# Layer 1's combine: the low half of a weight part one group of gathers later in GpSimd's program

## The reference

```
x = x + gnn(layernorm(x), adj)      # Wh = h @ W; masked softmax of (Wh@a1)_i + (Wh@a2)_j; elu(att @ Wh)
x = x + ffn(layernorm(x))           # router, top 2 of 8, out = sum over 2 experts of weight * (act(t@w1+b1)@w2+b2)
```

## Time and profile before

| | us |
|---|---|
| median of 3 runs | 1663.62 (1662.15 to 1683.7) |
| profiled execution, its own time | 1662.98 |
| its span, first to last instruction | 1661.2 |
| graph stage of layer 1 with the combine | about 578 to 930 |
| expert stage of layer 1 | about 1061 to 1580 |

### The profile page before, as it was taken

One profiled execution on the slowest core, in us unless ns is written; L12 is line 12 of the kernel. 1 busy time (PEld: TensorE's weight loads), 2 busy tenths in 40 slices (PEclk: granted clock), 3 DMA queues, 4 the chain that ended last, 5 costly groups with the idle time before them and its releaser, 6 DMA issues.

```text
span 1661.2 us, 31445 instructions
## 1 busy us (share of the span) xinstructions
PE 1157.8 (70%) x9230; PEld 923.0 (56%) x9231; DVE 992.0 (60%) x1742; ACT 554.3 (33%) x1103; POOL 751.4 (45%) x718
## 2 busy tenths in 40 slices
PE   5888481789999824545546563789989888989910
PEld 3666370478888712433435451477767676767710
DVE  3677698657777632555555798444444443434467
ACT  3776476222222213434446652022212221222200
POOL 2322274155555372444441473255656565655510
PEclk9999755589999956777778555589999998999965
DMA  8110141045555631222220341112222122212279
GB/s 246 47 33 14 45 175 53 14 133 158 163 160 164 149 104 45 60 67 64 64 64 14 127 165 38 39 64 71 74 73 80 66 75 69 76 66 73 67 261 364
DMA packets 124186, 161.23 MB, mean 97 GB/s; under 512 B 27352, under 2 KB 103648, under 8 KB 123872
## 3 DMA queue, kind: packets, MB, share of 16 engines
q1 hardware_dynamic: 97248, 87.10, 15.9%
q0 software_dynamic: 26880, 73.44, 14.9%
HBM read 97.57 MB, written 62.91 MB: 97 GB/s over the span
## 4 chain that ended last, share of the span: by engine, by line
PE 45%; issue 24%; DVE 9%; another core or an unknown queue 8%; DMA 4%; ACT 4%; POOL 3%; SPq 2%; DVEq 0%; ACTq 0%; POOLq 0%
PE bank L762 17%; PE bank L748 16%; PE bank L722 4%; PE bank L734 4%; DMA arena<-expert_outputs 2%; PE bank L607 2%; DVE X L1022 2%; PE bank L635 1%; DMA X<-in_x 1%; DVE stats L1012 1%; POOL stage_w L469 1%; ACT b_bc L814 1%; ACT arena L936 1%; POOL no_edge L478 1%
## 5 line engine op out<-in xcount | busy, mean ns | idle before, releaser
L552 POOL DMA_INDIRECT arena<-split_tokens,gather_row x288 | 288.8, 1003 | 234.2 <-DVE gather_row L1292 94.0
L936 ACT ACTIVATE arena<-bank,b1T 128x256 f32<-128x256 f32 x432 | 173.5, 474 | 629.5 <-PE bank L748 288.7
L762 PE MATMUL bank<-WREG,arena 128*128 x2592 | 332.8, 281 | 54.6 <-issue 35.5
L748 PE MATMUL bank<-arena,WREG 128*128 128x256 f16 x2592 | 327.1, 281 | 12.0 <-issue 11.3
L762 PEld LDWEIGHTS bank<-WREG,arena 128*128 128x128 f16 x2592 | 253.7, 100 | 113.7 <-issue 78.7
L748 PEld LDWEIGHTS bank<-arena,WREG 128*128 x2592 | 254.6, 101 | 51.6 <-issue 18.6
L1304 DVE CAST arena<-arena 128x512 f16<-128x512 f32 (+1 forms) x144 | 85.4, 593 | 250.9 <-ACT arena L936 196.7
L561 POOL DMA_INDIRECT expert_outputs<-arena,scatter_row x144 | 155.5, 1080 | 175.8 <-DVE arena L1317 145.7
L607 PE MATMUL bank<-wg_sb,arena 128*128 128x258 f32 x512 | 160.2, 459 | 93.1 <-issue 40.7
L607 PEld LDWEIGHTS bank<-wg_sb,arena 128*128 128x128 f32 x512 | 111.4, 229 | 125.7 <-issue 53.0
L494 POOL DMA_INDIRECT WREG<-expert_outputs,pos_i x128 | 124.3, 971 | 59.1 <-issue 36.9
(11 more groups left out here) (163 smaller groups left out, 1361.5 us busy)
## 6 DMA issues: line engine op xcount, KB each, us to landing
expert_outputs<-arena SPq DMA_DIRECT2D x72, 256.0 KB
split_tokens<-arena SPq DMA_DIRECT2D x32, 512.0 KB, 2.8
arena<-expert_outputs SPq DMA_DIRECT2D x32, 512.0 KB, 7.5
X<-in_x SPq DMA_DIRECT2D x16, 512.0 KB, 6.0
stage_w<-in_L_ffn_W SPq DMA_DIRECT2D x16, 512.0 KB
out<-X SPq DMA_DIRECT2D x16, 512.0 KB, 7.7
arena<-split_tokens,gather_row POOLq DMA_INDIRECT x288
stage_w<-in_L_ffn_w SPq DMA_DIRECT2D x16, 256.0 KB, 2.8
```

Of the source, the lines that this page charges most:

```text
L552: nc.gpsimd.indirect_dma_start(out=gat[:, u * 512:(u + 1) * 512], out_offset=None, in_=table[L], in_offset=bass.IndirectOffsetOnAxis(ap=ga ...
L748: last = mm(hb, w1_at(L, e, wh, kc, fc), tT[:, tb:tb + SLOT], start=n == 0, stop=n == 3 * KC - 1)
L762: last = mm(ob[a], hsrc[:, h0:h0 + P], w2_at(L, e, wh, fc), start=fc == 0 and n == 0, stop=fc == FC - 1 and n == 2)
L936: ins = A(hid[:, h0:h0 + SLOT], bank[2 + 2 * (u % 2) + fc // 2][:, (fc % 2) * SLOT:(fc % 2 + 1) * SLOT], ACT.Gelu if L == 0 else ACT.Relu, ...
```

## The change

Two conditions in POOL's program: the low half of part g-3, not of part g-2, is made behind the gathers of group g, and the last three lows, not two, follow the last gathers. No instruction is added or taken away.

```diff
                     for g in range(GROUPS):
                         gather_outputs(g)
-                        if g >= 2:
-                            low_part((g - 2) // 2, g % 2)
-                    for g in range(GROUPS - 2, GROUPS):
+                        if g >= 3:
+                            low_part((g - 3) // 2, (g - 3) % 2)
+                    for g in range(GROUPS - 3, GROUPS):
                         low_part(g // 2, g % 2)
```

## The result

The changed kernel takes 1692.21 us (median of 19 runs, 1671.81 to 1704.49), and the kernel before takes 1674.51 beside it (19 runs, 1662.15 to 1686.42). The ratio is 1.0084, 95% interval 1.0052 to 1.0116. The ratio leaves out runs more than 1.5% above the fastest of the same kernel, so it says less than the quotient of the medians. It is within 2%, but it is a loss, of some 14 us (0.0084 x 1674.5). The forecast of 1665 and its range up to 1677 were both too low.

What follows compares the result with a forecast made beforehand. The chain was PE's, with its completions held late while POOL issues gathers in bursts. Terms -0.7 (DVE's waits), -13.2 (iteration 5) and +16.2 (early burst) gave +2.3 on 1662.98, forecast 1665 us, range 1646 to 1677.

Steps and rivals of the forecast that it cites:

- hold: While POOL issues gathers back to back, PE's completions reach others late, coming out 2.9 to 5.5 us after the burst.
- DVE's waits, -0.7: DVE's ten waits for gathers (48.6 us) go, but are worth only -0.7 us, in iterations 1 and 4.
- Iteration 5, -13.2: Iteration 5 loses its burst and DVE sets the pace; soft(6) comes at 869.0 instead of 882.24: -13.2 us.
- The alternative of -18.0: Iteration 5 without its burst taking iteration 6's length, 24.3 us: -18.0, used only for the range.
- The early burst, +16.2: Prelude: group 3's gathers follow group 2's at once, 64 until 659.8; last scaling +14.9 to +17.5 us, middle +16.2.
- The weights, 0: Low halves still start when their high parts are there, so SP's loads keep their place: 0.
- The hold goes with DVE's waits: Rival: PE's results are late because DVE stands at a gather's semaphore; iterations 1 to 4 shrink, -55, 1610; chance 0.10.
- The early burst costs nothing: Rival: PE's prelude work keeps its own pace under the gathers, so +16.2 falls away: 1649; chance 0.12.
- Slower by more: Rival: 64 gathers in the prelude leave a longer backlog, ending one 11.2 us step later: 1676; chance 0.10.

Runs made afterwards that it cites:

- e5: The kernel before, unchanged, traced again on a chip with the hold: 1682.14 us.
- e6: The changed kernel again, on the same chip as e5: 1689.15 us, ratio 1.0089 to the kernel before.
- e11: Changed kernel with POOL's gathers replaced by as many plain copies of the same bytes from SP, chip with the hold: 1567.34 us (one run).
- set 2: The runs e5, e6, e7 and e8 on one chip with the hold, where the kernel before takes 1672.76 us.
- e7: Changed kernel with only group 3's gathers early and groups 4 to 7 at their old places: 1677.98 us, ratio 1.0037 to the kernel before.
- sets 1 and 4: Runs on two chips without the hold, where the kernel before takes 1528.27 and 1528.45 us.
- e3: Changed kernel with gathered rows of 64 bytes instead of 1 KB, same number of gathers, chip without the hold: 1486.61 us (one run).
- e16: Changed kernel with groups 2 and 3 waiting for PE's edges(0), no breaks, chip without the hold: 1477.09 us (one run).
- e10: The same kernel as e3 (64 byte rows), on a chip with the hold: 1693.59 us (one run).
- e12: Changed kernel with 3.4 us without a gather after every fourth gather, chip with the hold: 1650.14 us, ratio 0.9879 to the kernel before.
- e18: Changed kernel with a 1.3 us break after every fourth gather, chip with the hold: 1609.08 us, ratio 0.9618 to the kernel before.
- e8: Changed kernel with group 3's gathers held back until PE has done edges(0): 1681.16 us, ratio 1.0052 to the kernel before.
- e13: Changed kernel with a 1.3 us break after every fourth gather, chip without the hold: 1486.41 us, ratio 0.9720 to the kernel before.
- e15: The order of the kernel before with e13's 1.3 us breaks, chip without the hold: 1555.35 us, ratio 1.0170 to the kernel before.

## Why the prediction was wrong

The step that failed most is that the held iterations 1 to 4 keep their lengths but for DVE's waits (-0.7): the holds of iterations 1 and 4 doubled, and the two iterations became 6.4 us longer. The second is the term of the early burst, +16.2, which measured 17.9 to 19.8.

**DVE's waits, -0.7: the waits went, the iterations grew.** The waits went, and where PE set the pace they were worth nothing, as the prediction said (iterations 2 and 3: -0.4 and +1.4): ACT's hold took their place, 70.0 us of waits for L841 instead of 48.6 for gathers. Iterations 1 and 4 should have stayed where they were, and they became 3.3 and 3.1 us longer, because their hold went from 8.0 to 17.0 and 16.1. The forecast gave "about 3 us for an iteration that changes between 39 and 42 us" as scatter on both sides, and it took L625 to fall in the burst where it fell before (5.5 to 6.5 us in, by its end). That place moved a little. In the kernel before L625 began 4.41 and 4.42 us into the burst in iterations 1 and 4, and after the change 4.68 (715.60 against 710.91) and 5.61. The nine traces that have the hold and no breaks have 39 such short bursts. In 24 of them L625 began 4.5 us or later into the burst, and every one of these was held until 2.6 to 3.0 us after its end. In the other 15 (3.96 to 4.42) eight holds ended earlier, after 8.0 to 14.5 us, and seven did not. So a short hold was seen only with an early L625. Why, and what decides among the early ones, stays open.

**Iteration 5, -13.2: the mechanism right, the size nearly.** It was -11.8, and -9.4 in the pair of e5 and e6, where the kernel before had a shorter hold there (12.3 us). Its length is 30.5 us, that of any iteration with adds and no hold (30.6 in e11), where 29 was worked out. The alternative of -18.0 was too much, and so was the "about 15 to 20 us" that a burst was said to cost an iteration: it is 9 to 12.

**The early burst, +16.2: the mechanism right, the size too small.** The burst ended at 665.14 and ACT's slow results came as forecast, within 1 us, if the 5.6 us are added by which the first gather was later. But behind the result at 666.08 three tiles were left and not two: L806 at 671.68 and twice from 673.81. The last of them started at 674.4, where 665.1 to 667.7 was forecast, or 670.7 to 673.3 with the shift. By distance from the first gather the last scaling moved by 18.6 us, 2.4 more than the term. The other 1.2 us are the way from its end to soft(0), 6.1 us instead of 4.9. They come from the clock: the matmuls of edges(0), L614 and L615, took 3.78 us (from 677.29) and before 2.60 (from 653.06). In the windows of 11 us that end about there (us of PE, PEld, DVE, ACT and POOL with counts, then the granted clock, the DMA share and GB/s), before first:

```profile
645.00:656.00 11.00, 6.72 (x15) 3.97 (x16) 0.30 (x1) 5.07 (x15) 0.00 (x0) 0.66 0.01 2
```

and after:

```profile
671.00:682.00 11.00, 6.79 (x14) 3.71 (x15) 0.85 (x2) 4.14 (x14) 0.00 (x0) 0.50 0.00 1
```

After the change PE ran this stretch wholly at its lower level (0.50 is 1.2 of 2.4 GHz), where the trace of before has 0.66. But that isn't the change's doing. The second trace of the kernel before, e5, has the same window at the lower level too:

```profile
652.65:663.65 11.00, 7.64 (x14) 4.22 (x15) 0.04 (x1) 4.31 (x14) 0.00 (x0) 0.50 0.00 1
```

Its edges(0) took 3.78 us and its way to soft(0) 6.1, so that against e5 the clock plays no part. The term was 19.8, and 17.9 to 18.8 in set 2.

Two readings in this part of the prediction were wrong as well. 578.51 + 64 x 1.255 is 658.8 and not 659.8; the 64 gathers took 81.0 us (one in 1.265), so that the printed figure fitted by luck. And POOL wanted group 1's ring room 61.3 us after the first gather, at 639.8 in the times of before, not at 650. DVE's adds had ended at 625.56, so nothing hung on it.

**The weights, 0: nothing speaks against it.** The low halves show no cost: iterations 1 and 4 have the hold for their 3 us, and the others differ by -0.7 to +1.4 but for iteration 5. No run varied the low halves by themselves.

**The sum** was -0.7 - 13.2 + 16.2 = +2.3. It should have been +19.8 - 11.8 + 3.3 + 3.1 and +0.5 in small pieces (0.3 - 0.4 + 1.4 - 0.7, rounded), +14.9. The errors of the three terms are 3.6, 1.4 and 7.1 us, of one sign.

**The level** was a fourth. The forecast was tied to the 1662.98 of the profiled execution and to three runs, with a median of 1663.62. Nineteen runs have a median of 1674.51. The likely reason is the expert stage, which this change doesn't touch: it differs by some 20 us among the profiles of the changed kernel (501.0 to 521.4). The high end of the range, 1677, was only 2.5 us above the kernel before.

**The rivals.** *The hold goes with DVE's waits* (1610) fell with the trace of after: no wait for a gather in it, and four holds of 16 to 17 us. *The early burst costs nothing* (1649) fell with the prelude, +18 to +20 in four traces and e7. What the prediction drew from the Trainium skill (page "SBUF — State Buffer", section "SBUF: two separate sides"), that compute and DMA don't slow each other, doesn't hold for PE's completions in the traces with the hold. Whether the SBUF ports that the section speaks of have a part in it no run shows, so the section itself isn't refuted. In sets 1 and 4 the traces agree with it: L833 follows PE at once beside unbroken runs of 16 gathers and more (e3, e16), and the last scaling of the prelude starts 37 us after the first gather, under the 64 gathers of e3. *Slower by more* (1676) was the nearest in number, but not by its mechanism. Its mark was one more step of 11 us beyond the last gather. The slow step at 666.08 is the one that the forecast had at 659.6, and the next result, 671.68, came 5.6 us later. I had counted the tiles outstanding one too few, and the one more cost 2.4 us and not 11, since the burst's end released the rest.

**What is shown and what is not.** Shown, on the chips that have it: the hold needs the indirect gathers that POOL issues (e11), not their bytes (e10) and not DVE's waits (after), short breaks end it or nearly so (e12, e18), and it goes where the burst goes (e7, e8). Not shown: whether plain DMAs from POOL would make it too, what on the chip makes it, and why two chips lack it. Nor is it shown whether PE's work itself ends late or only word of it: the profile models the ends of matmuls. Each of these two was used in one set only, so the chip isn't told apart from the hour. The changed kernel itself was not run on a chip without the hold. It should be a gain there: e3, its order with thin rows, took 1486.61 against 1528.27, and e16, its order with whole rows and groups 2 and 3 held back, 1477.09 against 1528.45 (one run each). That is argued.

## What to carry to other kernels

An unexplained wait that is long whenever GpSimd issues many DMAs without a break is a reason to try breaking the run before reordering it: moving the burst cost 14 us, and a pause of 1.3 us after every four gathers took 76 us off the changed kernel (1684.71 to 1609.08). Where two limits lie side by side, here late gathers and the hold, an edit that takes away one of them shows nothing, or a loss; test it with the other one taken away as well (e13 against e15, 69 us, with breaks in both). And take the level of a forecast from more than three runs, if a stage that isn't touched moves by more than the effect.

## What the runs showed of the hardware

- While GpSimd issued indirect gathers every 1.25 us, PE's completions reached ACT 8 to 18 us after the end that the profile gives for the matmuls (0.05 us otherwise), and in a long burst at one in 11.2 us. Gathers of 64 byte rows did it as those of 1 KB, and a break of 1.3 us after every fourth gather limited it to under 4 us.
- In these runs it went with the chip: on two of them it occurred in no profile, and the kernel before took 1528 us there instead of 1670 to 1675. The expert stage differs too, by 92 to 114 us. PE's granted clock in its window is 1.00 in e13, where it takes 407 us:

```profile
996.00:1403.00 407.00, 405.96 (x3969) 363.86 (x3967) 221.45 (x283) 111.28 (x284) 308.42 (x277) 1.00 0.27 90
```

and 0.94 in e18, the same program on a chip with the hold, where it takes 499, with PE idle for 52 us of it:

```profile
1009.00:1508.00 499.00, 446.55 (x3965) 371.69 (x3964) 228.78 (x283) 111.50 (x284) 297.86 (x277) 0.94 0.22 73
```

POOL issues gathers and scatters all through this stage, so it may be the same hold; no run tested it there.
- The same matmuls of edges(0) took 3.78 us at a granted clock of 0.50 (after, e5) and 2.60 at 0.74 (before), each time behind a stretch in which PE had little to do (busy 8.0 of the 40 us from 605 before, 8.8 of the 55 us from 611 after).
